# A mixture of experts in two parts of its tokens: five groups' tiles beside the other three's dispatch, then the last tiles beside the first five's sums

## What is computed

```python
def _L1_ffn_ref(x, router_w, w_gate, w_up, w_down):       # 8 experts, D = 128, H = 256
    xt = x.reshape(-1, D)
    topk_vals, topk_idx = jax.lax.top_k(xt @ router_w.T, 2)
    g = jax.nn.sigmoid(topk_vals)
    g = g / (g.sum(axis=-1, keepdims=True) + 1e-10)
    out = jnp.zeros_like(xt)
    for e in range(8):
        ge = jnp.sum(jnp.where(topk_idx == e, g, 0.), axis=-1)
        h = jax.nn.silu(xt @ w_gate[e]) * (xt @ w_up[e])
        out = out + ge[:, None] * (h @ w_down[e])
    return out.reshape(B, S, D)
```

## Time and profile before

| | us |
|---|---|
| median of 3 runs (lowest to highest) | 2050.18 (2049.68 to 2053.37) |
| the profiled execution, its own time | 2051.13 |
| its span, first to last instruction | 2049.3 |
| mean granted clock of TensorE over the span | 0.919 |
| busy: PE, DVE, ACT, POOL | 1719.8, 1544.9, 1363.4, 877.9 |

### The profile page before, as it was taken

One profiled execution on the slowest core, in us unless ns is written; L12 is line 12 of the kernel. 1 busy time (PEld: TensorE's weight loads), 2 busy tenths in 40 slices (PEclk: granted clock), 3 DMA queues, 4 the chain that ended last, 5 costly groups with the idle time before them and its releaser, 6 DMA issues. The chain is left out here.

```text
span 2049.3 us, 39274 instructions
## 1 busy us (share of the span) xinstructions
PE 1719.8 (84%) x12410; PEld 1128.4 (55%) x12410; DVE 1544.9 (75%) x4156; ACT 1363.4 (67%) x4708; POOL 877.9 (43%) x816
## 2 busy tenths in 40 slices
PE   4999999999999955999999695999999683753991
PEld 2555555555555532777777352777777351552660
DVE  2898889988889965899999365899998365663445
ACT  2888888888888862888888222888888226322555
POOL 3555655555655543233233123233233123285555
PEclk9999999999999976999999896999999896755995
DMA  7990000000000000000000100000000100012324
GB/s 205 185 184 11 2 1 2 1 2 1 2 2 2 2 1 6 12 17 12 16 17 12 32 19 6 11 17 13 16 16 13 32 19 1 6 45 66 84 64 133
DMA packets 102525, 65.90 MB, mean 32 GB/s; under 512 B 27698, under 2 KB 93874, under 8 KB 102322
## 3 DMA queue, kind: packets, MB, share of 16 engines
q1 hardware_dynamic: 97970, 54.40, 13.3%
q0 software_dynamic: 4352, 8.99, 1.3%
HBM read 19.50 MB, written 30.24 MB: 24 GB/s over the span
## 5 line engine op out<-in xcount | busy, mean ns | idle before, releaser
L411 ACT ACTIVATE a_E<-a_psS,a_nm 128x128 f32<-128x128 f32 (+1 forms) x1028 | 419.9, 429 | 32.2 <-DVE a_nm L245 30.2
L216 POOL TENSOR_SCALAR a_aT<-a_dT 128x384 f32<-128x384 f32 x256 | 309.1, 1208 | 299.8 <-PE a_psO L529 187.6
L245 DVE TENSOR_REDUCE a_nm<-a_psS 128x2 f32<-128x256 f32 (+1 forms) x514 | 259.9, 546 | 43.9 <-PE a_psS L496 43.4
L492 PE MATMUL a_psS<-a_kT,a_qm 32*128 32x128 f32 (+1 forms) x2064 | 240.6, 351 | 5.4 <-issue 3.4
L270 DVE SCALAR_TENSOR_TENSOR a_d<-a_E,a_cf 128x128 f32<-128x128 f32 (+1 forms) x512 | 219.4, 468 | 27.9 <-DVE a_cf L259 1.4
L411 ACT ACTIVATION_READ_ACCUMULATOR a_E<-a_psS,a_nm 128x1 f32 x1028 | 220.7, 215 | 0.0
L830 POOL TENSOR_TENSOR b0rn<-b0ss,minus_half 128x16 f32<-128x16 f32 x36 | 107.2, 2977 | 223.6 <-DVE b0ss L866 223.6
L830 POOL TENSOR_TENSOR b1rn<-b1ss,minus_half 128x16 f32<-128x16 f32 x36 | 107.2, 2977 | 223.0 <-DVE b1ss L866 223.0
L420 ACT ACTIVATE a_dT<-a_psT 128x384 f32<-128x384 f32 x256 | 127.0, 496 | 73.9 <-PE a_psT L505 71.2
L492 PEld LDWEIGHTS a_psS<-a_kT,a_qm 32*128 32x128 f32 x2064 | 136.6, 186 | 55.9 <-issue 35.6
L505 PE MATMUL a_psT<-ident,a_d 128*128 128x128 f32 x768 | 132.6, 282 | 6.8 <-DVE a_d L270 1.0
(11 more groups left out here) (353 smaller groups left out, 4424.1 us busy)
## 6 DMA issues: line engine op xcount, KB each, us to landing
mx_rows<-mx_blank SPq DMA_DIRECT2D x9, 2080.0 KB, 31.2
mx_xin<-mx_rows SPq DMA_DIRECT2D x72, 65.0 KB
b0v<-b0v SPq DMA_DIRECT2D x34, 128.0 KB, 2.3
b1v<-b1v SPq DMA_DIRECT2D x34, 128.0 KB
F<-mx_results SPq DMA_DIRECT2D x8, 256.0 KB, 5.2
mx_second<-mx_results SPq DMA_DIRECT2D x8, 256.0 KB, 5.4
out_dram<-X SPq DMA_DIRECT2D x8, 256.0 KB, 2.3
f0z<-F SPq DMA_DIRECT2D x9, 128.0 KB
```

The lines of the kernel that those rows point to most:

```text
L216: pool.tensor_scalar(aT[:, s, :], dT[:, s, :], 0.0, None, ALU.max).then_inc(positived.sem, 1)
L245: ins = dve.tensor_reduce(nm[:, s, t, :], psS[:, s, :, (0, P)[t]:(P, 384)[t]], axis=AX.X, op=ALU.max, negate=True)
L411: ins = act.activation(E[:, s, m, c0:c1], psS[:, s, m, c0:c1], ACT.Exp, bias=nm[:, s, t, m:m + 1], accum_out=Z[:, p, h, t, m:m + 1])
L492: pe.matmul(psS[:, s, m, c0:c1], qm[rows, p, a, r, t * P:(t + 1) * P], kT[rows, p, a, 0:c1 - c0], start=(t == 0), stop=False)
```

## The change

The tokens are taken in two parts, groups 1 to 5 and 6 to 8 (`FIRST = (0, 5, GROUPS)`; in the code they count from 0). Each part has its own regions in `rows`, its own table (48 and 32 tiles, 80 in all), its own count of scatters and its own gates. The tiles of the first part stand in the queues ahead of the end of dispatch: GpSimd scatters six groups and half of the seventh before the first result, and the other twelve one behind every third result; the eighth group's route, choice, ranks and place, and the second table, lie between tiles 1 and 11. The five first groups' results are fetched by SyncE between the loads of tiles 66 and 67, and their sums lie between tiles 56 and 78, one group every four tiles (`SUM_AT`: 57, 61, 65, 69, 73); the addition to X of these groups is VectorE's and no longer GpSimd's. Results have eight buffers, not four (`YR`). PSUM is laid out anew: the turned h has one bank in place of two, and the rest of dispatch has banks of its own. The core of the diff:

```diff
+FIRST = (0, 5, GROUPS)
+PART_TILES = [NT * (FIRST[p + 1] - FIRST[p]) for p in range(2)]
+PART_SLOTS = [2 * n + NE for n in PART_TILES]
+START = [0, PART_SLOTS[0], sum(PART_SLOTS)]
...
-        psX = psG = ps("psG", [P, 2, 512])
-        psR = psH = ps("psH", [P, 2, 512])
-        psK = psY = ps("psY", [P, 2, 512])
-        psO = ps("psO", [P, 2, 512])
-        psT, psC = psO[:, 0, :], psO[:, 1, :]
+        psG, psY = ps("psG", [P, 2, 512]), ps("psY", [P, 2, 512])
+        psH, psT, psX, psR = ps("psH", [P, 512]), ps("psT", [P, 512]), ps("psX", [P, 512]), ps("psR", [P, 512])
+        psO = psY
+        psK, psC = psR[:, NT * NE:2 * NT * NE], psR[:, 2 * NT * NE:2 * NT * NE + NE]
...
+        LATE = GROUPS - 1
+        SUM_AT = {START[1] + 9 + 4 * g: g for g in range(FIRST[1])}
```

SyncE:

```diff
+            at = {}
+            for part in range(2):
+                sp.wait_ge(listed, part + 1)
+                for i in range(START[part], START[part + 1]):
+                    if i % SHARE == 0:
+                        _, values = nc.values_load_multi_w_load_instructions(
+                            c["place"][0:1, i:i + SHARE], engines=(mybir.EngineType.SP,), min_val=0,
+                            max_val=(NE + 1) * TILES * P - P, skip_runtime_bounds_check_because=BOUND)
+                        for k, v in enumerate(values):
+                            at[i + k] = v
+                    if i == START[part]:
+                        sp.wait_ge(sent[part], 16 * 2 * PART_TILES[part])
+                    if i >= RING:
+                        sp.wait_ge(x_full, (i - RING) // 2 + 1)
+                        sp.wait_ge(aimed, (i - RING) // SHARE + 1)
+                    load(i)
+                    if i == START[1] + RING + 2:
+                        fetch(0)
+            for g in range(FIRST[1] - 1):
+                store(g, done, g + 1)
+            fetch(1)
+            store(FIRST[1] - 1, done, FIRST[1])
+            for g in range(FIRST[1], GROUPS):
+                store(g, done_last, g - FIRST[1] + 1)
```

GpSimd:

```diff
-            for g in range(GROUPS):
-                send(g)
+            for g in range(LATE - 1):
+                send_group(g)
                 if g + 4 < GROUPS:
                     inner.power(pool, g + 4)
                 if g + 3 < GROUPS:
                     outer.power(pool, g + 3)
+            ready(LATE - 1)
+            for n in range(NT):
+                send(LATE - 1, n)
...
-                                        y[:, i % 4, :], None).then_inc(scattered[i % 4], 16)
+                                        y[:, i % YR, :], None).then_inc(scattered[i % YR], 16)
+                if i % 3 == 0 and i // 3 < 3 * NT:
+                    n = i // 3 + NT
+                    if n == 2 * NT:
+                        ready(LATE)
+                    send(LATE - 1 + n // (2 * NT), n % (2 * NT))
+                if i in SUM_AT:
+                    ln.power(pool, SUM_AT[i])
```

VectorE, in the dispatch loop, before the tiles, and in the tile loop:

```diff
+                place(g + 1)
+                if g + 2 == FIRST[1]:
+                    need_tiles(0)
+                    tiles_of_experts(0)
+                    rows_of_tiles(0)
+                residual(g + 3)
+            gates(0)
+            choose(LATE - 1)
+            place(LATE - 1)
+            outer.shifts(dve, LATE)
...
+                if i == 3:
+                    choose(LATE)
+                if i == 5:
+                    place(LATE)
+                if i == 7:
+                    need_tiles(1)
+                if i == 9:
+                    tiles_of_experts(1)
+                if i == 11:
+                    rows_of_tiles(1)
+                if i in SUM_AT:
+                    sum_results(SUM_AT[i])
+                if i - 3 in SUM_AT:
+                    ln.shifts(dve, SUM_AT[i - 3])
+                if i - 5 in SUM_AT:
+                    g = SUM_AT[i - 5]
+                    dve.wait_ge(normal, g + 1)
+                    dve.tensor_tensor(ln.tiles(X, g), ln.tiles(X, g), second[:, of(g), :], ALU.add).then_inc(done, 1)
```

ScalarE, in the tile loop:

```diff
+                if i + 1 in SUM_AT:
+                    weigh(SUM_AT[i + 1])
+                if i - 3 in SUM_AT:
+                    normal_apply(SUM_AT[i - 3])
                 move_h(i)
```

TensorE, before the tiles, in the tile loop, and in the turn of h:

```diff
             pe.wait_ge(listed, 1)
             load_experts(0)
+            route(LATE - 1)
+            ranks(LATE - 1)
+            turn(LATE)
...
+                if i == 1:
+                    route(LATE)
+                if i == 4:
+                    ranks(LATE)
...
             def turn_h(i):
                 pe.wait_ge(h_ready, i + 1)
-                if i >= 2:
-                    pe.wait_ge(hT_ready, i - 1)
+                if i >= 1:
+                    pe.wait_ge(hT_ready, i)
```

More of the change, by code:

```diff
@@ L1587, in _ @@
         def _(sp):
[L1588 to L1599, removed]
-                  .then_inc(landed[i % RING], 16)
@@ L1602, in _, with load @@
-            for k in range(4):
-                sp.wait_ge(scattered[k], 16 * (SLOTS // 4))
-            o = out.rearrange("b (t p) d -> p (b t) d", p=P)
-            for g in range(GROUPS):
-                sp.dma_start(ln.tiles(F, g), result(0, g)).then_inc(fetched[g], 16)
-                sp.dma_start(second[:, of(g), :], result(1, g)).then_inc(fetched[g], 16)
-            for g in range(GROUPS):
-                sp.wait_ge(done, g + 1)
-                sp.dma_start(o[:, of(g), :], ln.tiles(X, g)).then_inc(stored, 16)
+            def load(i):
+                sp.dma_start(xin[:, i % RING, :], rows[bass.ds(at[i], P), :]).then_inc(landed[i % RING], 16)
@@ new lines, in fetch, with store @@
+            def fetch(part):
+                for k in range(YR):
+                    sp.wait_ge(scattered[k], 16 * (START[part + 1] // YR))
+                for g in range(FIRST[part], FIRST[part + 1]):
+                    sp.dma_start(ln.tiles(F, g), result(0, g)).then_inc(fetched[g], 16)
+                    sp.dma_start(second[:, of(g), :], result(1, g)).then_inc(fetched[g], 16)
+            def store(g, ready, count):
+                sp.wait_ge(ready, count)
+                sp.dma_start(o[:, of(g), :], ln.tiles(X, g)).then_inc(stored, 16)
@@ L1618, in send, with send_group @@
                 pool.sem_inc(held, 1)
-                for t in range(NT):
-                    for choice in range(2):
-                        pool.indirect_dma_start(
-                            rows, bass.IndirectOffsetOnAxis(ap=posu[:, g, choice, t:t + 1], axis=0),
-                            pay[:, g * NT + t, :], None).then_inc(sent, 16)
+            def send(g, n):
+                t, choice = divmod(n, 2)
+                pool.indirect_dma_start(
+                    rows, bass.IndirectOffsetOnAxis(ap=posu[:, g, choice, t:t + 1], axis=0),
+                    pay[:, g * NT + t, :], None).then_inc(sent[part_of(g)], 16)
+            def send_group(g):
+                ready(g)
+                for n in range(2 * NT):
+                    send(g, n)
             for g in range(LEAD):
@@ L1812, in _ @@
             place(0)
-            for g in range(GROUPS):
-                if g + 2 < GROUPS:
-                    outer.shifts(dve, g + 2)
-                if g + 3 < GROUPS:
-                    inner.shifts(dve, g + 3)
-                if g + 1 < GROUPS:
-                    choose(g + 1)
+            for g in range(FIRST[1]):
+                outer.shifts(dve, g + 2)
+                inner.shifts(dve, g + 3)
+                choose(g + 1)
                 if g + 4 < GROUPS:
                     outputs(g + 4)
-                if g + 1 < GROUPS:
-                    place(g + 1)
-                if g + 3 < GROUPS:
-                    residual(g + 3)
-            tiles_of_experts()
-            gates()
+                place(g + 1)
[8 more added lines that the diff above has]
+            outer.shifts(dve, LATE)
             gate_up(0)
```

235 lines of the change are left out of this document (136 added, 99 removed).

## The result

The changed kernel is slower: a median of 2075.05 us (2068.70 to 2077.22, 4 runs) beside 2051.69 for the kernel before (4 runs), a ratio of 1.0109 (95% interval 1.0084 to 1.0134). The forecast was 2038, range 2027 to 2050. Of the 37 us between, 1.5 is that before's median stood at 2050.18 when the forecast was made. The profiled execution took 2068.70 us, its span is 2066.9.

A forecast was written before the change was run, and what follows sets the result against it. Took GpSimd's scatter queue to bound dispatch and TensorE the tiles after it. Terms -28.3 + 13.1 + 4.0 + 14.4 - 15.5 = -12.3 us, from 2050.2 to 2037.9, said as 2038; range 2027 to 2050.

The forecast's parts named there:

- Step 1: Start of the tiles: first-part tiles need only five groups' scatters, so they start 28.3 us earlier, bounds 25 and 32.4.
- (b): Before the first tile: TensorE's queue holds the seventh group's ranks and the eighth's turn, so tiles start at 1855.1.
- a late signal on VectorE: Rival: VectorE's unexplained 9.4 us wait beside unbroken scatters recurs once in full on the path; 2047 us, chance 0.10.
- Step 2: Tile run: 48 and 32 tiles replace 72, eight more at 1.64 us, +13.1 us, bounds 13 and 14.
- 1.64 us a tile from tile 5 to 55: Sign in the tile run: after the wait at tile 4, tiles keep this pace until the rounds with sums.
- step 6: Terms costing nothing: five groups' fetches ahead of loads, and dispatch's last twelve scatters, 5.1 us in 4.9, lag carried by buffers.
- Step 3: First tiles: the last group's routing inside them costs +4.0 us, including a +1.8 stall for the choice; bounds 2 and 8.
- Step 4: Last 24 tiles: sums of five groups among them stall TensorE, +14.4 us; lower bound 2, upper 27.
- the rival: TensorE's clock: stalls in rounds with sums drop it from 1.00 to 0.50, +23 us, 2061 us; chance 0.09.
- the 2.5 us left to the range: Sums among tiles: each of five 0.5 us longer beside GpSimd's power through SBUF contention; not put in the sum.
- Step 5: Tail: three groups of eight are left to sum and normalise, -15.5 us, bounds 13 and 16.
- at about 2007: Sign at the end of the tiles: the last result's time, with 29.6 us from it to the end.

The follow-up runs named there:

- before_again: The kernel before, unchanged, run once more with a profile: 2048.3 us in one run, beside 2048.6 for before in that job.
- before_shifted: The kernel before plus 160 unused bytes a partition of SBUF ahead of dispatch's constants and five unused semaphores: 2053.9 us beside 2045.8, ratio 1.0041.
- changed_third: The changed kernel itself, unedited, profiled a third time: 2053.5 us in one run, beside 2048.5 for before in that job.
- compute_again: The changed kernel with GpSimd memsets of 1.2 us in place of the twelve scatters among the tiles, repeated: 2059.4 us in one run, before there 2051.0.
- two_banks: The changed kernel with two banks for the turned h, as before the change: 2047.5 us, beside 2048.7 for before in that job.
- no_sends: The changed kernel without the twelve scatters of dispatch among the tiles: 2053.3 us, beside 2048.7 for before in that job.
- sums_behind: The changed kernel with all eight groups' sums behind the last tile and GpSimd making every last addition: 2043.5 us, before there 2048.7.
- padded: The changed kernel with an unused SBUF tensor of 96 bytes a partition ahead of dispatch's constants: 2047.7 us, beside 2048.5 for before in that job.

## Why the prediction was wrong

*Step 1, the earlier start.* The chain (b) was right: the first transpose at 1856.1 against 1855.1, and on chips of the fast kind the first result 27.2 us earlier against 28.3. On a chip of the slow kind 18 to 22. What failed is the use of the earlier trace rows: VectorE's wait of 9.43 us there was taken for a chance event, the rival "a late signal on VectorE", priced once and given 0.10. It looks like the mechanism that decides this case: the wait is as long on a chip of the slow kind and short on one of the fast kind, in one profile each. The same wait, first before_again (chip 5), then before_shifted (chip 11):

```profile
1863.88 0.19 DVE L1710 TENSOR_TENSOR mx_rank<-mx_psY,mx_region 128x32 f32<-128x32 f32 x1 [8.20 <-remote]
```
```profile
1863.34 0.19 DVE L1713 TENSOR_TENSOR mx_rank<-mx_psY,mx_region 128x32 f32<-128x32 f32 x1 [1.96 <-PE mx_psY L1962]
```

*Step 2 and the pace.* The failed step is "1.64 us a tile from tile 5 to 55" with step 6's "at nothing" for dispatch's last twelve scatters. It holds on four chips (-0.3 us over 40 tiles, on chip 10 with the scatters spaced) and fails in the three other jobs by 11.9 to 16.1. GpSimd's share was computed (5.1 us of scatters in 4.9 of tiles) and only its lag was asked for, not what an unbroken row of scatters does to others.

*Step 3*, +4.0, measured +5.0 between results 0 and 12; with the twelve scatters +6.8 to 8.6 on the slow kind. The stall for the choice of tile 4, +1.8 in the forecast, is there; changed_third, TensorE:

```profile
1874.67 0.36 PE L2065 MATMUL mx_psR<-mx_seen,mx_ones 128*128 128x8 f32 x2 [1.73 <-DVE mx_seen L1761]
```

*Step 4*, +14.4, measured 14.1 with two banks and 18.7 with one. The stall itself is nearly as worked out; changed_third, TensorE in one round (predicted 2.25):

```profile
1995.15 0.41 PE L2110 MATMUL mx_psH<-ident,mx_h 128*128 128x128 f32 x2 [2.01 <-ACT mx_hT L1979]
```

What it left out is that the clock gives way in part with one bank: the rival had 23 us from a clock of 0.50, and it came as 4.6 us in 20 tiles, at a mean of 0.88. Where the clock stays at 1.00 with one bank, two rounds each in the changed kernel's first profile and in compute_again (1990 to 2010) take 9.2 to 9.3 us, as with two banks. So the 4.6 us are the clock's, not a wait for the bank. That the second bank keeps the clock up rests on the kernel two_banks: its mean clock was 0.924 to 0.928 in ten runs, that of no_sends on the same chip 0.920 to 0.924. And the sums were no bargain: moved behind the tiles (sums_behind) they cost 7.9 us at the end and save 18.7.

One reading in this step was wrong, and nothing in the sum hung on it. What GpSimd did beside the VectorE instruction of 0.65 us (2022.32) was not its power, which began at 2023.04, but the addition to X; before, GpSimd:

```profile
2021.67 1.26 POOL L1651 TENSOR_TENSOR X<-X,mx_second 128x512 f32<-128x512 f32 x1 [0.63 <-ACT mx_second L647]
```

The five groups' additions to X are VectorE's now, so the 2.5 us left to the range had no ground.

*Step 5*, -15.5, measured -12.0. The span ends 8.8 us after GpSimd's last addition in the changed kernel and 6.2 in the one before, with nothing in the trace between but the last store. Five semaphores more don't make it (before_shifted: 6.2), twelve scatters fewer take 1.0 off (7.8 to 7.9 in all five such profiles); the cause stays open. The last result "at about 2007" and "29.6 us" behind it did not come out of the forecast's own sum either, which gives 2009.0 (2005.8 + 3.2) and 28.0.

*Outside all steps*, the start of the block: +3.1 to +6.4 us in layers whose code is the same, the 3 to 8 us of the address, with what these profiles happened to be ahead or behind at 1130 us (-3.0 to +1.4). The forecast took for granted that a block's change stays in the block.

Put together, for changed_third (chip 12, a chip of the fast kind, without late signals): +5.6 -27.2 +5.0 -0.3 +31.2 -11.9 = +2.4 us, where -12.3 was forecast; of the 14.7 us between, 5.6 is the start of the block (7.1 from the address, less 1.5 of chance ahead of it), 4.6 the clock in the rounds with one bank, 3.6 the end, 1.1 step 1 and 1.0 step 3 (less 1.2 of small change). On a chip of the slow kind 21 more come on top (medians 2074.4 and 2075.1 against the 2053.5 of changed_third), the larger part of the 37 us of the miss. That scatters bring them about is shown by one job, on chip 0, with one profile of each kernel; how they do it, and why only in some jobs, stays open.

## What to carry to other kernels

Do not take a wait whose input was long done for noise before a second chip has been tried: ask what ran beside it, and whether your change puts more of that beside the path. Try a change in more than one job, with the unchanged kernel beside it, and keep the changed kernel itself in every job of experiments. When constants ahead of other layers change size, keep the change of their total a multiple of 256 bytes a partition, or look at the transfers of the layers that you did not touch.

## What the runs showed of the hardware

- In three of seven jobs (chips 5, 0, and one without a number) VectorE and ScalarE start 1 to 3 us after the signal that they waited for, while GpSimd issues indirect scatters 0.30 us apart; in the three others where unbroken rows ran among the tiles (chips 7, 12, 11) not in these stretches, with the same code there and the same gaps. On chip 0 tiles 12 to 52 took 16 us more than before with the twelve scatters, 2 with memsets of 1.23 us in their place and 1 with nothing there.
- 160 bytes of shift make SBUF-to-SBUF transfers into f0z 1.2 us longer at the first wait (11.45 to 12.62) and put 5.8 to 8.1 us on a 2048 us program (padded against changed_third, before_shifted against before). The feed-forward's four such waits come to 31.0 us in before_again and 35.3 in before_shifted.
- With stalls of TensorE of 2.0 us in rounds of four tiles its granted clock was 0.83 to 0.84 in each 10 us (no_sends and padded, 1970 to 2010), a mean of time at 1.00 and time at 0.50, and a round took 10.5 us in place of 9.3.
